# Expert outputs added into row sums in memory by accumulating indirect transfers, then copied to the output

## The reference

```python
xn = _layernorm(x)
# dense branch: attention over windows, x2 = layernorm(xn + attn), y = x2 + gelu(x2 @ W1 + b1) @ W2 + b2
# expert branch, comb = weights of the two best experts of each token, zero elsewhere
def step(acc, p):
    uw, ub, gw, gb, dw, db, w = p
    h = jax.nn.silu((xf @ gw.T + gb) * (xf @ uw.T + ub))
    return (acc + w[:, None] * (h @ dw.T + db), None)
return x + dense(xn) + y_experts
```

## Time and profile before

| what | value |
|---|---|
| median of 3 runs | 1272.08 us |
| lowest, highest | 1269.12, 1273.16 us |
| the profiled execution, its time | 1271.41 us |
| the profiled execution, its span | 1269.6 us |
| mean granted TensorE clock | 0.937 |
| dense stage ends, expert stage begins | at about 619 us |
| last expert transfer issued | at about 1231 us |

### The profile page before, as it was taken

The page is one execution under the profiler, slowest core; times in us unless marked ns, Lnnn a source line. Parts: engine busy times, 40 slices in busy tenths (PEclk is TensorE's granted clock), DMA queues, the critical chain, the costliest instruction groups (busy, mean ns, idle before and its releaser), DMA issues.

```text
span 1269.6 us, 30066 instructions
## 1 busy us (share of the span) xinstructions
PE 1107.0 (87%) x9070; PEld 1025.2 (81%) x9070; DVE 881.5 (69%) x2032; ACT 851.2 (67%) x1994; POOL 636.8 (50%) x910
## 2 busy tenths in 40 slices
PE   2878898989897979888999999999999999999950
PEld 2866686868686868777889999999999999998950
DVE  7566564647465655656678888888888888888825
ACT  2455766768585857586578877777778878877720
POOL 6013543232232314052167777777777777776740
PEclk8588898989898999999999999999999999999985
DMA  8870011010101010031341111125411241125119
GB/s 285 278 225 26 30 35 51 21 45 25 42 29 37 33 37 33 26 131 35 104 153 31 33 33 33 36 79 173 150 53 33 91 145 31 33 87 198 43 51 347
DMA packets 68338, 106.72 MB, mean 84 GB/s; under 512 B 7693, under 2 KB 60046, under 8 KB 66640
## 3 DMA queue, kind: packets, MB, share of 16 engines
q1 hardware_dynamic: 60704, 86.55, 21.1%
q0 software_dynamic: 7600, 19.74, 4.4%
HBM read 138.52 MB, written 37.50 MB: 139 GB/s over the span
## 4 chain that ended last, share of the span: by engine, by line
PE 32%; ACT 26%; DVE 21%; issue 15%; DMA 2%; SPq 2%; DVEq 1%; ACTq 0%; POOL 0%; POOLq 0%
PE bank L1204 7%; PE bank L1205 6%; PE bank L1206 6%; ACT hf L792 6%; DVE gu_s L1123 5%; DVE gu_s L1130 4%; ACT sm L695 4%; ACT gs L785 3%; DVE hf L1143 3%; PE bank L1301 3%; PE bank L1329 2%; ACT gu_s L803 2%; DVE ys L1159 2%; PE bank L1291 2%; ACT ht L796 2%
## 5 line engine op out<-in xcount | busy, mean ns | idle before, releaser
L1204 PE MATMUL bank<-xt_h,gu_s 128*128 128x256 f32 (+1 forms) x1014 | 293.2, 289 | 23.4 <-DVE hf L1143 20.8
L1205 PE MATMUL bank<-xt_l,gu_s 128*128 128x256 f32 (+1 forms) x1014 | 287.3, 283 | 0.0
L1206 PE MATMUL bank<-xt_h,gu_s 128*128 128x256 f32 (+1 forms) x1014 | 286.7, 283 | 0.0
L620 POOL TENSOR_TENSOR ht<-hf,ht 128x256 fp32r<-128x256 f32 (+1 forms) x273 | 240.1, 891 | 70.8 <-ACT ht L796 61.0
L1130 DVE TENSOR_TENSOR gu_s<-raw_gu,gu_s 128x512 fp32r<-128x512 f32 (+1 forms) x273 | 203.2, 767 | 64.0 <-ACT gu_s L803 63.9
L1204 PEld LDWEIGHTS bank<-xt_h,gu_s 128*128 128x128 f32 (+1 forms) x1014 | 192.1, 189 | 30.5 <-issue 27.6
L1206 PEld LDWEIGHTS bank<-xt_h,gu_s 128*128 128x128 f32 (+1 forms) x1014 | 192.1, 189 | 0.0
L1205 PEld LDWEIGHTS bank<-xt_l,gu_s 128*128 128x128 f32 (+1 forms) x1014 | 191.8, 189 | 0.0
L792 ACT ACTIVATE hf<-hf 128x256 f32<-128x256 f32 (+1 forms) x273 | 113.4, 415 | 85.9 <-DVE hf L1143 81.5
L695 ACT ACTIVATE sm<-sm,least 128x256 f32<-128x256 f32 x256 | 126.9, 499 | 30.4 <-DVE least L973 30.1
L611 POOL TENSOR_TENSOR dw_s<-raw_dw,dw_s 128x256 fp32r<-128x256 f32 x117 | 108.4, 952 | 70.7 <-ACT dw_s L810 70.2
(11 more groups left out here) (177 smaller groups left out, 2812.6 us busy)
## 6 DMA issues: line engine op xcount, KB each, us to landing
raw_gu<-in_gu_dram SPq DMA_DIRECT2D x39, 1648.0 KB
raw_dw<-in_dw_dram SPq DMA_DIRECT2D x39, 768.0 KB
xs_dram<-zrec SPq DMA_DIRECT2D x6, 1677.0 KB, 14.4
xr<-xs_dram SPq DMA_DIRECT2D x39, 258.0 KB, 2.8
yg<-y_dram SPq DMA_DIRECT2D x16, 512.0 KB, 8.3
xwin<-xn_dram SPq DMA_DIRECT2D x8, 640.0 KB, 4.8
raw_dw<-in_dw_dram SPq DMA_DIRECT2D x78, 64.0 KB
xg<-in_x_dram SPq DMA_DIRECT2D x8, 512.0 KB, 6.3
```

Of the source, the lines that this page charges most:

```text
L620: nc.gpsimd.tensor_tensor(low, hf[0:m, ring(c), :], ht[0:m, p, 0, c, :].bitcast(F32), ALU.subtract).then_inc(h_split, 1)
L1204: nc.tensor.matmul(dst, lhs[0], rhs[0], start=start, stop=False)
L1205: nc.tensor.matmul(dst, lhs[0], rhs[1], start=False, stop=False)
L1206: return nc.tensor.matmul(dst, lhs[1], rhs[0], start=False, stop=stop)
```

## The change

- `y_dram` is gone. `sum_dram` has one row for each token and 256 rows more for padding.
- SP stores each group's dense sums from `xn` to `sum_dram` (`store_sum`): seven in the dense turns, behind the load of `xres` and ahead of the load of the window, and the last one at the start of the expert stage, behind the down weights of block 1.
- POOL waits before block 0 until all eight stores have landed.
- `send` adds its rows to `sum_dram` in the transfer itself (`compute_op=ALU.add`). Since two blocks can hold the same token, it first waits until the two transfers of the block before have landed.
- The token number in a record is the same for both choices. Padding names one of the 256 extra rows, each once in a block, and is really transferred. For this `zrec` has two versions.
- The end is eight copies of 512 KB from `sum_dram` to the output, from memory to memory, with no add and nothing on chip.

```diff
@@ program @@
-    y_dram = nc.dram_tensor("y_dram", (2 * S, D), F32, kind="Internal").ap()
+    sum_dram = nc.dram_tensor("sum_dram", (S + BT, D), F32, kind="Internal").ap()
...
-        zrec = tile("zrec", [REC])
+        zrec = tile("zrec", [2, REC])
...
-        fourth, tile = phase()
-        yg = tile("yg", [YB, 2, GT, D])
-        fourth.close()
@@ sync @@
+            def store_sum(g):
+                sp.dma_start(sum_g[ds(g, 1)].rearrange("o p t d -> p (o t) d"), xn[:, ds(g * GT, GT), :]).then_inc(sum_stored, 16)
...
                 load_residual(at.g)
+                store_sum(at.f)
...
             load_gu(2, 0)
             load_dw(1, 1, False)
+            store_sum(NG - 1)
             load_rows_of(2, 0)
...
             sp.wait_ge(y_sent[0], 32 * ((NB + 1) // 2))
             sp.wait_ge(y_sent[1], 32 * (NB // 2))
-            def load_rows(g, p):
-                for k in range(2):
-                    sp.dma_start(yg[:, p, k], y_dram[ds(g * GN + k * S, GN), :].rearrange("(t p) d -> p t d", p=P)).then_inc(yg_loaded[p], 16)
-            def store_out(g):
-                sp.wait_ge(sum_2, g + 1)
-                settle(sp)
-                sp.dma_start(out_g[ds(g, 1)].rearrange("o p t d -> p (o t) d"), xn[:, ds(g * GT, GT), :]).then_inc(out_stored, 16)
...
+            for g in range(NG):
+                sp.dma_start(out[g * GN:(g + 1) * GN, :], sum_dram[g * GN:(g + 1) * GN, :]).then_inc(out_stored, 16)
             sp.wait_ge(out_stored, 16 * NG)
@@ gpsimd @@
-            nc.gpsimd.iota(zrec[:, D:D + 1].bitcast(I32), [[0, 1]], base=2 * S, channel_multiplier=1).then_inc(zrec_ready, 1)
+            nc.gpsimd.iota(zrec[:, :, D].bitcast(I32), [[P, 2]], base=S, channel_multiplier=1).then_inc(zrec_ready, 1)
...
             def send(b, p):
                 pool.wait_ge(y_ready, b + 1)
+                if not isinstance(b, int) or b >= 1:
+                    settle(pool)
+                    pool.wait_ge(y_sent[1 - p], (b + p) * 16)
                 settle(pool)
                 for t in range(2):
                     index = dest[:, 2 * p + t:2 * p + t + 1]
-                    nc.gpsimd.indirect_dma_start(y_dram, bass.IndirectOffsetOnAxis(index, 0), ys[:, p, t, :], None,
-                                                 bounds_check=2 * S - 1, oob_is_err=False).then_inc(y_sent[p], 16)
+                    nc.gpsimd.indirect_dma_start(sum_dram, bass.IndirectOffsetOnAxis(index, 0), ys[:, p, t, :], None,
+                                                 bounds_check=S + BT - 1, compute_op=ALU.add).then_inc(y_sent[p], 16)
...
+            pool.wait_ge(sum_stored, 16 * NG)
             blocks_of(pool, body)
@@ vector @@
-            def add_rows(g, p, n):
-                dve.wait_ge(yg_loaded[p], n * 32 + 32)
-                span = xn[:, ds(g * GT, GT), :]
-                nc.vector.tensor_tensor(span, span, yg[:, p, 0], ALU.add).then_inc(sum_1, 1)
-                dve.wait_ge(sum_1, g + 1)
-                nc.vector.tensor_tensor(span, span, yg[:, p, 1], ALU.add).then_inc(sum_2, 1)
```

More of the change, by code:

```diff
@@ L266, in program @@
         y_sent = sems("y_sent_0 y_sent_1")
[L267 to L268 removed]
+        sum_stored, out_stored = sems("sum_stored out_stored")
         x_g = x.rearrange("(g t p) d -> g p t d", t=GT, p=P)
[L271 removed]
+        sum_g = sum_dram[0:S, :].rearrange("(g t p) d -> g p t d", t=GT, p=P)
         DENSE = [(wq, wq_s, KC, D), (wk, wk_s, KC, D), (wv, wv_s, KC, D), (w1, w1_s, KC, F1), (w2, w2_s, FC1, D)]
@@ L358, in _ @@
             sp.wait_ge(zrec_ready, 2)
-            sp.dma_start(xn_dram[0:WIN, :], zrec[0:WIN, 0:D]).then_inc(pads_filled, 16)
-            sp.dma_start(xn_dram[WIN + S:PADROWS, :], zrec[0:WIN, 0:D]).then_inc(pads_filled, 16)
+            sp.dma_start(xn_dram[0:WIN, :], zrec[0:WIN, 0, 0:D]).then_inc(pads_filled, 16)
+            sp.dma_start(xn_dram[WIN + S:PADROWS, :], zrec[0:WIN, 0, 0:D]).then_inc(pads_filled, 16)
             def store_xn(g):
@@ L904, in route_weights @@
                 for k in range(2):
-                    link(nc.vector.tensor_scalar(meta[:, k, :, 0].bitcast(I32), cst[:, C_TOK:C_TOK + NT], float(k * S), None, ALU.add))
+                    link(nc.vector.tensor_copy(meta[:, k, :, 0].bitcast(I32), cst[:, C_TOK:C_TOK + NT]))
             def route_starts(at):
@@ L1186, in _ @@
             weigh(NB - 1, (NB - 1) % 2)
-            def add_rows(g, p, n):
-                dve.wait_ge(yg_loaded[p], n * 32 + 32)
-                span = xn[:, ds(g * GT, GT), :]
-                nc.vector.tensor_tensor(span, span, yg[:, p, 0], ALU.add).then_inc(sum_1, 1)
-                dve.wait_ge(sum_1, g + 1)
-                nc.vector.tensor_tensor(span, span, yg[:, p, 1], ALU.add).then_inc(sum_2, 1)
-            with dve.Fori(0, NG // YB) as i:
-                for p in range(YB):
-                    add_rows(i * YB + p, p, i)
         @block.tensor
```

22 lines of the change are left out of this document (5 added, 17 removed).

## The result

| kernel | median, us | lowest, highest | profiled execution | its span |
|---|---|---|---|---|
| before, on the same chip | 1270.6 | 1268.66, 1273.16 | 1271.41 | 1269.6 |
| changed | 1331.46 | 1328.53, 1334.96 | 1328.53 | 1326.6 |

The changed kernel is **slower by a factor of 1.048** (95% interval 1.0445 to 1.0513): 61 us, not 8. The forecast was 1279.7, with 1326 as the upper end.

The account below looks back on a forecast made before the run. It took TensorE to bound the expert stage and transfers alone the end. End -10.4, start +8.3, sends +4.4 and landing +6 sum to +8.3: span 1277.9, time 1279.7 us, range 1258 to 1326.

Parts of the forecast that it names:

- the term for the sends on POOL: Each block: two issues 0.2 us longer plus 0.08 for a wait, less 0.36 spare, 0.12 x 37 = 4.4 us.
- the landing: Each block: `keep_meta` waits for sends landing at 4.1 us instead of 2.7; 6 us in all (0 to 12).
- the added wait: POOL's wait for the previous send before each send: only its own instruction, 0.08 us a block.
- the slack: Time POOL has to spare before DVE's multiply of chunk 3 must wait for its first `h_low`: 0.36 us a block.
- The start: Start of expert stage: POOL's first `h_low` waits for the last group's store, delay passed on in full, 8.3 us.
- The end: After the last send: final loads, adds and stores replaced by a 4.19 MB copy at 184 GB/s, -10.4 us.
- The rival with the fast copy: End copy at the DMA engines' 368 GB/s, -21.8 us, issue also within POOL's spare time: 1259.9 us, chance 0.22.
- What costs nothing: Dense-turn stores, longer `zrec` and second iota under first loads, DVE's adds, padding rows in other blocks: no cost.
- POOL as the bound: Rival in the blocks: accumulating issue doubled, sends cost 64 us, +68 in all, 1339 us; chance 0.20.
- The rival with the issue in the slack: Accumulating issue at most 0.14 us longer, so sends cost nothing: +0.9 us, 1272.3 us, no change; chance 0.22.

Follow-up runs that it names:

- the kernel with `keep_meta` late: Changed kernel with stores' wait ahead of first send, block b-2's send behind `h_low` 2, paired fills, `keep_meta` behind `h_low` 6: 1276.63 us, ratio 1.0035.
- the run with the stride alone: Kernel before, with its six record-table fills going to every other 128 slots from the same short source: 1281.23 us (one run).
- the split behind `h_low` 0 and 2: Changed kernel with late sends, paired fills and `keep_meta` behind `h_low` 6, a send's first transfer behind `h_low` 0, second behind 2: 1285.59 us, ratio 1.0126.
- the moves alone, without the accumulation: Kernel before with padding records in pairs, send of block b-2 behind `h_low` 2, `keep_meta` behind `h_low` 6: 1263.47 us, ratio 0.9938.
- the kernel with memsets: Kernel before with a memset of 128 x 280 numbers on POOL behind each issue of a send, except in the last block: 1292.24 us, ratio 1.0159.

## Why the prediction was wrong

- **The step that failed** is the term for the sends on POOL, 4.4 us. Together with the landing (6 us) the sum had 10.4 us for the blocks; 66.8 were measured behind the stall at the start. Two things were wrong in it.
- **Its mechanism, the larger part.** The sum treated GpSimd as a queue, and VectorE as losing only what GpSimd is late beyond a slack. What the runs showed is VectorE's cast of chunk 3 shut out over three `h_low`, 3.16 us instead of 0.96: at least 1.37 us a block or some 50 us, as an estimate. The prediction had come near it: from the Trainium skill (SBUF — State Buffer, SBUF: two separate sides) it took a VectorE cast that holds up GpSimd's descriptors, priced it at 10 us from rows 4, and left it out of the sum. The loss is on the other side, the cast waits. The same page says in another section (Who interferes with whom) that whoever issues first gets the shared pair for the whole instruction and the other fully blocks. The trace agrees that one side is fully blocked, but it stays so over three instructions and not one, though the cast's row starts ahead of theirs (703.63 against 703.82). None of rows 4 shows the cast. The trace of the kernel before would have warned, by the one cast of 1.87 us at 1162.51 shown above.
- **Its size.** It took 0.2 us more for each issue from POOL's plain transfers; the rows are 0.55 us longer, though only the first one's 0.55 reaches `h_low`. By the prediction's own formula that is 0.55 + 0.08 - 0.36 = 0.27 us a block, x 37 = 10 us instead of 4.4. Neither of the other two numbers held: the added wait cost nothing (GpSimd idled 0.16 us before the first issue, in the kernel before 0.15), and the slack was nearer 0.2 than 0.36, since `h_low` 0 took 1.24 us and not a third of its row of three.
- **The range.** Its upper end of 1326 us was said to be an issue 0.7 us longer. By the prediction's own sum that gives 1317, and 1326 needs 0.83. So that it came within 5 us of the measured 1331 is luck: the loss came by another way.
- **The start.** Taken at 8.3 us (4.6 to 9), it was 9.2 at the first blocks, just outside, and 6.9 over the stage. The mechanism was as described.
- **The landing.** 4.1 us in the median, as forecast, and 26.0 us of waits instead of 12.4. No loss of its own can be told: the stage lost 66.8 us behind the start stall, less than 37 quiet blocks would (37 x 1.97 = 73), and with the wait taken off POOL's path (in the kernel with `keep_meta` late) the block gained 0.1 us.
- **The end.** Forecast -10.4 us, measured -19.9. What is removed and added was right, and the copy's rate mis-sized: 339 GB/s and not 184. The sum had taken the memory, which each byte crosses twice, as the limit at 368 GB/s; it was not. The rival with the fast copy had it (21.8).
- **What costs nothing.** The fills were put there, under the first loads, and only for their source. They cost 6.6 us in the profiled execution, where the DMA engines are full (1.08 to 1.10) and the first pass waits for them; the run with the stride alone shows 8.9 us.
- **The rivals.** POOL as the bound (1339) is nearest in time, but by luck, as its terms were others: the issue did not double, the landing took 4.1 us in the median, and POOL is busy for 49% of the span, before for 50%. The rival with the issue in the slack fell, and so did the fast copy's total of 1260.

As a sum: +1.0 (6.6 of fills, -4.4 by an earlier start of that stretch, -1.2 in the dense turns, within what executions differ), +9.2, +66.8, -19.9 = +57.1.

## What to carry to other kernels

A new operation on an engine is not priced by its length alone: look at what the neighbouring engine starts before it ends, and how many operations stand behind it in a row without a pause. A long operation of the neighbour in that place can wait for all of them. Idle time of the issuing engine is not enough as a rule: the split behind `h_low` 0 and 2 had it too, and lost. Try the places, since moving one of two issues by one operation was worth some 30 us here, and one operation further lost 40. With the other moves it made of a change that lost 61 us one that gains 25, of which the moves alone, without the accumulation, give 7. And where a stretch is bound by transfers, the order of the addresses in a fill is part of its price.

## What had not been expected of the hardware

- A VectorE rounding that starts while an issue or a memset of GpSimd still runs, with a row of `h_low` behind that, can be shut out over all of them: 3.16 us for a cast that takes 0.41 alone, 3.41 for a two-input maximum. Plain issues do it too (1.87 us). A cast that began 0.57 us after the start of the row, with the issue over, took 0.96. In the kernel with memsets either side won (14 to 22). What decides it was not found.
- An accumulating indirect transfer of 128 rows of 1 KB takes 1.54 to 1.83 us of GpSimd to issue by its row, a plain one 0.99 to 1.27, but GpSimd's next operation starts beside the last half us of it; it lands after 4.1 us in the median, a plain one after 2.7.
- A copy from memory to memory in pieces of 32 KB ran at 339 GB/s.
- Fills in pieces of 1032 B ran at 336 to 342 GB/s in order, at 253 to 288 when each transfer skips every other 132 KB, and pairs of 2064 B in order at 380.
